# Three units of a set turned in blocks instead of two, with other places for attends, copies, stores and loads, in a four-layer graph network on one core

## What is computed

```python
x = layernorm(x + gru(relu((adj @ x) @ W_msg.T + b_msg), x))     # layer 0
x = layernorm(x + D (adj + I) D (x @ W) + b)                     # layer 1, D = rowsum(adj + I) ** -0.5
# layer 2: attention with 4 heads of 32, masked where adj == 0
q, k, v = x @ Wq + bq, x @ Wk + bk, x @ Wv + bv
e = exp(where(adj == 0, -inf, q k^T / sqrt(32)) - rowmax);  o = (e / rowsum(e)) v
x_r = x @ Ws + bs;  beta = sigmoid([o, x_r, o - x_r] @ Wb)
x = layernorm(x + beta * x_r + (1 - beta) * o)
# layer 3: hyperbolic convolution
xt = logmap0(proj(mobius_add(mobius_matvec(W, x), bias)))
x = layernorm(x + relu-and-maps(adj @ xt))
```

## Time and profile before

| | us |
|---|---|
| median of 3 runs | 1786.05 |
| range of the 3 runs | 1782.78 to 1787.19 |
| the profiled execution | 1782.96 |
| its span, first to last instruction | 1781.3 |

### The profile page before, as it was taken

The page is one execution under the profiler, slowest core; times in us unless marked ns, Lnnn a source line. Parts: engine busy times, 40 slices in busy tenths (PEclk is TensorE's granted clock), DMA queues, the critical chain, the costliest instruction groups (busy, mean ns, idle before and its releaser), DMA issues.

```text
span 1781.3 us, 40266 instructions
## 1 busy us (share of the span) xinstructions
PE 1735.9 (97%) x15000; PEld 1131.3 (64%) x15000; DVE 1228.6 (69%) x2405; ACT 975.8 (55%) x1505; POOL 895.6 (50%) x849
## 2 busy tenths in 40 slices
PE   7999999999998999999999999999999999999996
PEld 3444444444444778877877887778778777644442
DVE  4777775222225889999999999999999999301322
ACT  0110111010103898999999999999999999411101
POOL 0212120112114755778878788788787896540211
PEclk9999999999998999999999999999999999999998
DMA  9866676899996544445445445454454543897981
GB/s 382 325 221 251 254 252 224 278 313 371 332 366 184 186 155 161 155 155 167 150 140 182 150 152 170 156 173 150 142 178 144 167 157 116 323 371 275 321 323 57
DMA packets 134029, 388.53 MB, mean 218 GB/s; under 512 B 15712, under 2 KB 66144, under 8 KB 109280
## 3 DMA queue, kind: packets, MB, share of 16 engines
q1 hardware_dynamic: 117792, 356.11, 57.6%
q10 hardware_dynamic: 13824, 22.75, 3.6%
q0 software_dynamic: 2240, 7.34, 1.6%
HBM read 333.19 MB, written 52.95 MB: 217 GB/s over the span
## 4 chain that ended last, share of the span: by engine, by line
PE 92%; DVE 4%; issue 1%; ACT 1%; DMA 1%; POOL 1%; DVEq 0%; ACTq 0%; POOLq 0%; SPq 0%
PE bank L592 35%; PE bank L742 23%; PE bank L763 14%; PE bank L701 13%; DVE arena L1281 2%; PE bank L580 1%; PE bank L655 1%; PE bank L614 1%; PE bank L613 1%; DMA arena<-x_dram 1%; PE bank L607 0%; PE bank L769 0%; PE bank L650 0%; PE bank L789 0%; PE bank L630 0%
## 5 line engine op out<-in xcount | busy, mean ns | idle before, releaser
L976 ACT ACTIVATE arena<-arena,small 128x2048 f32<-128x2048 f32 x256 | 516.2, 2016 | 2.8 <-DVE small L1281 2.8
L742 PE MATMUL bank<-ident,arena 128*128 128x128 f32 x3592 | 485.5, 278 | 4.4 <-ACT arena L976 2.6
L742 PEld LDWEIGHTS bank<-ident,arena 128*128 128x128 f32 x3592 | 398.1, 141 | 87.8 <-issue 41.9
L592 PE MATMUL bank<-arena,stat_s 128*128 128x512 f32 x1008 | 439.1, 592 | 2.1 <-issue 1.2
L988 ACT ACTIVATE arena<-bank 128x512 f32<-128x512 f32 x673 | 377.0, 604 | 66.2 <-PE bank L742 65.3
L701 PE MATMUL bank<-k,parts 128*128 128x512 f32 x1024 | 354.4, 436 | 10.6 <-DVE small L1281 10.6
L592 PEld LDWEIGHTS bank<-arena,stat_s 128*128 128x128 f32 x1008 | 189.2, 190 | 226.8 <-issue 225.4
L763 PE MATMUL bank<-arena,stat_x 128*32 128x128 f32 x8192 | 276.5, 276 | 0.0
L763 PEld LDWEIGHTS bank<-arena,stat_x 128*32 128x32 f32 x8192 | 208.1, 109 | 90.8 <-issue 81.5
L592 PE MATMUL bank<-arena,stat_x 128*128 128x512 f32 x512 | 228.3, 598 | 10.1 <-DMA arena<-adj_cols 7.8
L701 PEld LDWEIGHTS bank<-k,parts 128*128 128x128 f32 x1024 | 158.8, 192 | 29.6 <-DVE small L1281 24.5
(11 more groups left out here) (155 smaller groups left out, 1431.8 us busy)
## 6 DMA issues: line engine op xcount, KB each, us to landing
arena<-adj_cols SPq DMA_DIRECT2D x190, 1024.0 KB, 6.4
stat_s<-adj SPq DMA_DIRECT2D x85, 512.0 KB, 4.8
group_dram<-stat_s SPq DMA_DIRECT2D x63, 512.0 KB, 2.9
arena<-group_dram SPq DMA_DIRECT2D x252, 128.0 KB, 2.8
arena<-adj SPq DMA_DIRECT2D x43, 512.0 KB, 4.6
parts<-q_dram SPq DMA_DIRECT2D x128, 64.0 KB, 2.4
k<-k_dram POOLq DMA_DIRECT2D x28, 256.0 KB, 9.5
x_dram<-arena ACTq DMA_DIRECT2D x16, 256.0 KB, 3.7
```

The costliest lines, as they stand in the source:

```text
L592: mm_ = pe.matmul(bank[:, to, :], stat[:, jt, :], ring[:, s, j, :], start=(jt == 0), stop=(jt == TILES - 1))
L742: last = pe.transpose(bank[:, b_, h * P:(h + 1) * P], cols[:, st % SETS, h, u * P:(u + 1) * P], ident[:, :])
L976: act.activation(cols[:, s_, h, :], cols[:, s_, h, :], ACT.Exp, bias=shift[:, t % 2, 1, i:i + 1], scale=-1.0, accum_out=blocksum[:, t % 2, ...
```

## The change

- Units 13, 14 and 15 of a set form the group; VectorE turns them in blocks at places 1, 2 and 6 of the set (before: 14 and 15 at places 3 and 5). A chunk has 104 units left for TensorE to turn; 23 of them are copied by VectorE and 81 by ScalarE. The store of a group has 768 KB, each of its four loads 192 KB.
- The attends of a set are issued in three batches: four at place 4 (the last four of the set before), six at place 8, six at place 14.
- The eight slots of copies no longer share space with the groups. The group's own three slots lie in `stat_s`, and its load waits until the last set's group has been attended.
- Adjacency rows have two buffers, not three. SP's order per set is group store, mask load, group load, mask load, queries.
- `SPILLED` is chunks 0 to 5. GpSimd issues their stores itself, right after xt. At the end xt of chunks 0, 1 and 5 is loaded ahead of the first four ring slots, xt of 2, 3 and 4 behind them; the product waits for the first three at its start and for the rest after slot 1.
- Places of exponentials move. Of the steps after a chunk, blend goes from GpSimd's step 9 to 8, the statistics on VectorE from 41 and 45 to 42 and 46, its last norm from 113 to 115, ScalarE's last logarithms from 119 to 121.

```diff
-ATTEND_BATCH = 4
-ATTEND_LAG = 8
-BLOCK_TURN_AT = {14: 3, 15: 5}
-GROUPS = ((14, 15),)
-VECTOR_PLACES = (6,)
+ATTENDS = {4: (-4, -3, -2, -1), 8: (0, 1, 2, 3, 4, 5), 14: (6, 7, 8, 9, 10, 11)}
+BLOCK_TURN_AT = {13: 1, 14: 2, 15: 6}
+GROUPS = ((13, 14, 15),)
+VECTOR_PLACES = ()
+VECTOR_ALSO = (5, 6, 7, 19, 25, 27, 38, 54, 58, 59, 66, 69, 82, 86, 87, 91, 92, 97, 99, 103, 119, 121, 123)
+VECTOR_NOT = ()
...
-MASK_AHEAD = 8
-MASKS = 3
-SPILLED = (2, 3, 4, 5)
+MASK_AHEAD = 7
+MASKS = 2
+SPILLED = (0, 1, 2, 3, 4, 5)
+FIRST_XT = (0, 1, 5)
+OTHER_XT = (2, 3, 4)
...
+def slot_of(k):
+
+    return (PE_UNITS + LAST_UNITS).index(k) % TURNED
+
+
+def used_before(c, k):
+
+    i = (PE_UNITS + LAST_UNITS).index(k) - TURNED
+    return c * UPC + PE_UNITS[i] + 1 if i >= 0 else (c - 1) * UPC + PE_UNITS[i] + 1
...
-        group_slots = arena[:, RING + 10 * CHUNK:RING + 12 * CHUNK]
...
-        adj_in = (arena[:, RING + 4 * CHUNK:RING + 6 * CHUNK], spilled[:, 0:2 * CHUNK], spilled[:, 2 * CHUNK:4 * CHUNK])
...
+        adj_in = (arena[:, RING + 4 * CHUNK:RING + 6 * CHUNK], spilled[:, 0:2 * CHUNK])
+        group_slots = spilled[:, 2 * CHUNK:5 * CHUNK]
+        blocks = [stat_s[:, TILES - 3 * TPC:TILES, :].rearrange("p t f -> p (t f)")]
...
-                if g * UPS + GROUPS[i][-1] >= TURNED:
-                    sp.wait_ge(unit_used, g * UPS + GROUPS[i][-1] - TURNED + 1)
+                if g > 0:
+                    sp.wait_ge(unit_used, (g - 1) * UPS + GROUPS[i][-1] + 1)
...
-                    load_mask_ahead(c, 2 * st + 0)
                     if g < GROUP_SETS:
                         store_group(g, 0)
-                    if st == 0 and c - 2 in SPILLED:
-                        store_xt(c - 2)
+                    load_mask_ahead(c, 2 * st - 1 if g == 0 else 2 * st)
                     if g < GROUP_SETS:
                         load_group(g, 0)
+                    if g == 0:
+                        load_mask_ahead(c, 2 * st)
+                    load_mask_ahead(c, 2 * st + 1)
...
-                    load_mask_ahead(c, 2 * st + 1)
...
                 if c == CHUNKS - 1:
+                    load_first_xt()
                     load_ring(2, 0, True, range(4))
+                    load_other_xt()
                 load_residuals(c)
...
+            def load_other_xt():
+                sp.wait_ge(unit_used, GROUP_SETS * UPS)
+                load_xt(OTHER_XT, xt_in_place)
...
-                    if (k - ATTEND_LAG) % ATTEND_BATCH == 0:
-                        for a in range(k - ATTEND_LAG, k - ATTEND_LAG + ATTEND_BATCH):
-                            if a >= 0:
...
+                    for a in attended_at(c, k):
+                        if a >= 0:
...
+            pe.wait_ge(first_xt_in, 16 * len(FIRST_XT))
...
+                    if c in SPILLED:
+                        pool.wait_ge(att_pool, AG(c, "xt"))
+                        pool.dma_start(xt_dram[c - SPILLED[0], :, :], mx_g).then_inc(xt_out, 16)
...
-                return {4: beta_terms, 6: residual_terms, 9: blend, 11: rs, 14: x3sq, 17: mx_terms, 19: norms,
+                return {4: beta_terms, 6: residual_terms, 8: blend, 11: rs, 14: x3sq, 17: mx_terms, 19: norms,
```

More of the change, by code:

```diff
@@ L483, in attention_loads, with load_xt, load_first_xt @@
                 if c == CHUNKS - 1:
+                    load_first_xt()
                     load_ring(2, 0, True, range(4))
+                    load_other_xt()
                 load_residuals(c)
-            def store_xt(c):
-                sp.wait_ge(att_pool, AG(c, "xt"))
-                sp.dma_start(xt_dram[c - SPILLED[0], :, :], mx_g).then_inc(xt_out, 16)
-            def load_xt():
+            def load_xt(chunks, landed):
+                for i in chunks:
+                    sp.dma_start(spilled[:, i * CHUNK:(i + 1) * CHUNK], xt_dram[i, :, :]).then_inc(landed, 16)
+            def load_first_xt():
                 sp.wait_ge(bias_ready, CHUNKS * COLS)
@@ L494, in load_xt @@
                     sp.wait_ge(group_out[i], 16 * GROUP_SETS)
-                for i in range(len(SPILLED)):
-                    sp.wait_ge(xt_out, 16 * (i + 1))
-                    sp.dma_start(spilled[:, i * CHUNK:(i + 1) * CHUNK], xt_dram[i, :, :]).then_inc(xt_in_place, 16)
+                sp.wait_ge(xt_out, 16 * len(SPILLED))
+                load_xt(FIRST_XT, first_xt_in)
+            def load_other_xt():
+                sp.wait_ge(unit_used, GROUP_SETS * UPS)
+                load_xt(OTHER_XT, xt_in_place)
             def load_residuals(c):
@@ L815, in attention @@
                 if last_chunk:
-                    for a in range(UPC - ATTEND_LAG, UPC):
+                    for a in range(UPC - 4, UPC):
                         attend(c, a, first)
@@ L981, in copy_unit @@
                 if not (first and k < TURNED):
[L982 to L988 removed]
+                    act.wait_ge(unit_used, used_before(c, k))
+                elif k >= TURNED - 2:
+                    act.wait_ge(gcn_x2_out, 16 * CHUNKS)
+                elif k >= TURNED - 4:
+                    act.wait_ge(gcn_k_out, 32 * CHUNKS)
+                act.activation(turned[slot_of(k)], bank[:, unit_bank(k), :],
                                ACT.Copy).then_inc(unit_copied_act, 1)
@@ L1372, in norm_h @@
                     dve.tensor_reduce(hh, tiles(y_g), AX.X, ALU.add).then_inc(att_dve, 1)
-                return {25: beta_logit, 33: gate, 41: stats, 45: lambda: mean_and_var(att_dve, AV, c),
+                return {25: beta_logit, 33: gate, 42: stats, 46: lambda: mean_and_var(att_dve, AV, c),
                         55: norm, 63: norm_x3, 73: norm_mx, 77: bias_mx, norm_h_at: norm_h}
             def attention(c, first, last_chunk):
-                post = post_steps(c - 1, 107 if last_chunk else 113) if not first else {}
+                post = post_steps(c - 1, 107 if last_chunk else 115) if not first else {}
                 for k in range(UPC):
```

74 lines of the change are left out of this document (31 added, 43 removed).

## The result

The changed kernel takes 1775.26 us (median of five runs, 1772.95 to 1779.95), the kernel before 1786.05 us (1782.78 to 1787.19). The ratio is 0.9947, with a 95% interval of 0.9929 to 0.9965: 10.8 us faster, about half of the 20.9 us that the sum gave. The time is inside the stated range and outside the forecast's own range (1757 to 1773); it is in that of rival 3, the gain eaten by late data.

The account below looks back on a forecast made before the run. TensorE was taken to bound the attention stage, VectorE close behind. Six chunks at 2.7 us, chunk 0 at 4.5 and chunk 7 at 2.7, less seams of 1.5 and 1, gave 20.9 us: 1765 us, range 1750 to 1784.

Parts of the forecast that it names:

- rival 3: Attention stage: group or GpSimd chain late by 0.2 to 0.4 us a set, 1773 to 1787 us; chance 0.20.
- the bound: Attention stage: TensorE sets the pace at 119.86 us a chunk, its busy time being real work, not padding.
- the group's way round: Group's store to HBM and loads back: hidden, 7.3 us against 1.75 of issue and some 4 of landing; priced at nothing.
- the two mask buffers: Mask loads, two buffers for three: late masks don't reach VectorE; 0, bounds -0.4 to +1 us a chunk.
- VectorE as second: Attention stage: VectorE some 6.5 us a chunk behind TensorE before; its demand becomes 115.3 us.
- Coupling of two equal engines: Attention stage: TensorE and VectorE wait for each other, 1.8 us a chunk, bounds 0.3 and 6.5, giving 117.2 us.
- the terms 3.3 and 1.2: TensorE's savings a chunk: 3.3 us from unit 13 turned by VectorE, 1.2 us from one batch of attends fewer a set.
- Rival 2: Attention stage: VectorE's work sets the pace and its 6.5 us of waits stay; 121.8 us a chunk, 1802 us; chance 0.08.
- The signs: Wrong if VectorE idles 4 us a chunk, attends wait for DMA, or the first product starts over 3 us later.
- GpSimd's own stores: Spilled features of six chunks stored by GpSimd: 0, at most +2 us a chunk on GpSimd, which has 17 us slack.
- moved places: Steps after a chunk: blend earlier, statistics, last norm and logs later give GpSimd's chain about two places; priced at 0.
- The seams: Start and end of the attention stage: +1.5 us (0 to +3) at the start, +1 us (0 to +4) at the end.

Follow-up runs that it names:

- the run with both: Changed kernel with a third mask buffer (every third mask load 256 of 1024 columns) and smaller group stores and loads; 1759.27 us, one run.
- the third buffer: Changed kernel with a third mask buffer, every third mask load bringing 256 of 1024 columns; 1766.49 us, ratio 0.9895 against the kernel before.
- the light group: Changed kernel storing a quarter of the group's bytes and loading a third of them, same number of DMAs; 1765.54 us, one run.
- the kernel with light masks: Changed kernel with two mask buffers, each mask load bringing 256 of 1024 columns, group DMAs whole; 1770.29 us, one run.

## Why the prediction was wrong: two terms priced at nothing

The direction and the bound were right; the gain was about half of what the sum gave. What failed are two terms that stood at 0, the group's way round and the two mask buffers. By the runs that make these paths light, data that come late on them cost about 2.1 us a chunk.

**The bound, and VectorE as second.** That TensorE's busy time before was real work held: it has 3340 turns and the chunk did get shorter by taking some away. VectorE's demand was put at 115.3 us a chunk; it is 688.12 / 6 = 114.7. The Trainium skill ("Perfetto Trace Analysis", Identifying the Most-Contended Engine) would have VectorE (96.5% busy in the six chunks, TensorE's weight loads 79%) optimised first. Read so, the chunk should follow VectorE's work. Measured: 2.7 us of that work gone, 0.17 us of the chunk gone. The trace doesn't agree with the rule.

**Coupling of two equal engines** was put at 1.8 us a chunk, an estimate between 0.3 and 6.5. With little late data the chunk is 116.75 us, 1.35 over the 115.4 that the sum had as TensorE's demand. That is the forecast's term, 0.45 us smaller, if 115.4 is right. TensorE's busy time speaks for it: 716.96 / 6 = 119.5 us a chunk before, 689.78 / 6 = 115.0 in the run with both, 4.5 less, which is what the terms 3.3 and 1.2 add up to. It doesn't tell the two apart. Rival 2 (121.8 us, VectorE's work sets the pace) falls by the run with less work on VectorE.

**The step that failed: the group's way, priced at 0 with "1.5 us to spare".** The store of 768 KB landed after 4.1 us and the loads after 3.7; forecast were 4.5 and some 4. The Trainium skill ("DMA: Bandwidth & Descriptors", Anatomy of one DMA) gives 2.0 us plus the bytes at 436 GB/s, for transfers that GpSimd issues: an estimate of 3.8 us for 768 KB and 3.2 for 512 KB. SP's stores took 4.1 and 3.0; the trace agrees to 0.3 us. The durations of the typical transfer were not the error. TensorE's and SP's timelines of one set, and the landing line of the loads:

```profile
1154.56 1.52 PE L782 MATMUL bank<-arena,stat_x 128*32 128x128 f32 x48
...
1160.23 1.52 PE L782 MATMUL bank<-arena,stat_x 128*32 128x128 f32 x48
...
1165.25 0.84 PE L782 MATMUL bank<-stat_s,stat_x 128*32 128x128 f32 x24
```

```profile
1154.46 0.34 SPq L463 DMA_DIRECT2D group_dram<-stat_s  x1
1154.84 0.43 SPq L445 DMA_DIRECT2D stat_s<-adj  x1
1158.56 1.74 SPq L474 DMA_DIRECT2D stat_s<-group_dram  x4
```

```profile
DMA to landing us min/median/max: 2.7/3.7/5.8
```

I counted the store's start in VectorE's places ("leaves after place 6") and the deadline in TensorE's (place 20). The two engines are not at the same place at the same time: the store leaves at 1154.46, as TensorE begins the attends of its place 8 at 1154.56. That is about one place later than I had it, and a store that lands 0.4 us sooner makes up for part of it. The loads are issued from 1158.56 to 1160.30 and the attends that need them stand at 1165.25, 6.7 us after the first load, where I had 7.3. After the issue 4.95 us are left for a landing of 3.7, so this set has 1.2 us to spare.

The typical set was thus priced nearly right. What I left out is the spread: I set one median against another. Read from the two timelines for all 48 sets of the six chunks, the first attend of a group stands 3.6 to 6.6 us after the end of the issue (median 5.1), and the loads land 2.7 to 5.8 us after theirs. Where a short cover meets a long landing nothing is left, and in 7 to 11 of the 48 sets an attend waits (the last two rows of the waits above: 7 waits and 4). Making the group light is worth 1.28 us a chunk, 1.10 where the third buffer is there already.

The matching rows understate it. Attends wait for the group for 4.1 us in six chunks by the profile, 0.7 a chunk. The rest may stand in other waits, such as copies and scores that meet late; no row shows which.

**The second step that failed: two mask buffers at 0.** I priced by places for the masks ("neither reaches VectorE"). What comes later is GpSimd's chain after a chunk, for which the post steps on VectorE and ScalarE wait: 13.0 us in six chunks, while the rows with the third buffer have no such wait. The bound of 1 us a chunk was about the truth in the changed kernel (0.98 with the caveat above); in the kernel before, buffers and SP's order together cost 2.06. Rival 3 named both causes with 0.33 us a set; they cost 2.08 / 8 = 0.26 us a set. Its time was added up wrongly: 0.2 to 0.4 us over 64 sets on 1765 is 1778 to 1791, not 1773 to 1787.

**The signs.** I named three by which I would be wrong. VectorE idles for 4.1 us a chunk ((712.90 - 688.12) / 6), and attends wait for DMA: two came true. The third did not, since the first product of the last layer follows the last attends at once (they end at 1532.67, it starts at 1532.60). The first sign alone would have spoken for rival 2 as well; only the run with less work on VectorE took that away.

**GpSimd's own stores, moved places:** no run takes them away alone, so their 0 wasn't tried by itself. In the trace each store costs GpSimd a wait of about half a microsecond and an issue of 0.7, six times, against 19.5 us of idle a chunk ((712.90 - 595.67) / 6; the prediction's 15% and 17 us were too low already for the kernel before, where 98.45 of 120 us leave 18%). Two more places for the post steps changed nothing.

**The seams.** The Mobius product of a chunk stands in the middle of the next, so the forecast's parts are cut there. Between the traces all up to the first of these products (chunk 0 and half of chunk 1) gave 763.19 - 761.28 = 1.9 us, where 4.5 + 1.35 - 1.5 = 4.35 were forecast; the first turn of the stage is 2.1 us later, 580.51 against 578.41, so the stage itself gave 4.0 up to there. The six chunks gave 6.2 us of 16.2. From the seventh Mobius product to the end the changed kernel is 0.4 us longer, where 1.35 - 1 = 0.35 us less was forecast. The first product of the last layer starts 13.8 us after the first ring loads (14.4 before; forecast about 14), but the last group of all makes an attend wait 1.63 us. TensorE's and SP's timelines at the end:

```profile
1521.85 0.86 PE L782 MATMUL bank<-stat_s,stat_x 128*32 128x128 f32 x24 [1.63 <-DMA stat_s<-group_dram]
...
1532.60 3.70 PE L612 MATMUL bank<-arena,stat_s 128*128 128x512 f32 x8
```

```profile
1518.84 2.07 SPq L424 DMA_DIRECT2D arena<-adj_cols  x4
```

**In all:** forecast -2.7 us a chunk, measured -1.03. Had the two late paths been priced with their 2.08 us and the coupling with 1.35, the sum would have given 115.4 + 1.35 + 2.08 = 118.83 us; over the eight chunks 8 x (2.08 - 0.45) = 13 us less gain, -8 us, against -7.7 between the traces and -10.8 between the medians. This closes because both terms were read from runs of the same kernel; it is no proof of either. The 2.08 us were measured by taking bytes away, so they hold what the lighter traffic does for other transfers as well.

**Open:** the worth of three batches alone, and why four of them cost 4.1 us a chunk in the changed kernel. How the mask path's 0.98 us divides between buffer and bytes is not settled either, nor how the 2.06 us in the kernel before divide between buffers and SP's order.

## What to carry to other kernels

Where data go round by HBM between two engines, take the time that is left from a row of each engine at the same moment, since places of a hand-written order are not simultaneous on different engines. Then set the shortest cover against the longest landing, not one median against another: 1.2 to 1.4 us to spare in the typical set still left 7 to 11 sets of 48 late. When engines are balanced to a few per cent, price lateness by making the transfer light, not by the wait rows: these showed 0.7 us a chunk where the light transfer gave 1.1 to 1.3, and cutting the work of the engines that they name most gave 0.2 us. See what else the light transfer speeds up. Before taking a buffer away, follow the engine that fills from it down to its last consumer; GpSimd had 19.5 us of idle a chunk and still made others late.

## What the runs showed of the hardware

Transfers slow each other in this stage. With the light group the mask loads, whose 512 KB are untouched, land after a median of 4.1 us instead of 5.1. And with light masks beside the whole group the mask loads still take 4.0 us: 128 KB among the group's whole transfers land hardly sooner than 512 KB among light ones. The group's own loads did not gain by the light masks (3.7 us both times). The landing lines of the mask loads, of the light-group kernel and then of the kernel with light masks:

```profile
DMA to landing us min/median/max: 3.5/4.1/6.1
```

```profile
DMA to landing us min/median/max: 2.1/4.0/5.9
```

A DMA share of 0.67 was enough for this; the DMA engines looked a third idle in the mean. TensorE's clock was at 1.00, its full 2.4 GHz, in every window above, also where it stood still for 3 us a chunk.
